# An attention kernel at one head and batch row per period: one load moved in ScalarE's queue, the weights' low parts given to GpSimd, and two planes made a stage earlier

## The reference

```python
x = x + _L0_cond_ref(x, adapter_ids, weight)      # x + x @ weight[id].T, per batch row
...
q = _rope(_rmsnorm(einsum('bsd,ed->bse', x, Wq), q_norm_w), pos)
k = _rope(_rmsnorm(einsum('bsd,ed->bse', x, Wk), k_norm_w), pos)
v = einsum('bsd,ed->bse', x, Wv)
k_all, v_all = [cached pages (512 keys), new keys (128)]
scores = einsum('bqhd,bkhd->bhqk', q, k_all) / sqrt(128); masked beyond the cached length
x = x + softmax(scores) @ v_all, through Wo
```

## Time and profile before

| what | us |
|---|---|
| median of 3 runs | 1062.12 |
| lowest and highest of them | 1061.57, 1069.5 |
| profiled execution, its own time | 1067.74 |
| its span in the trace | 1065.6 |
| TensorE busy in the span | 1021.3 |
| VectorE, ScalarE, GpSimd busy | 867.0, 804.7, 756.6 |

### The profile page before, as it was taken

One profiled execution on the slowest core, in us unless ns is written; L12 is line 12 of the kernel. 1 busy time (PEld: TensorE's weight loads), 2 busy tenths in 40 slices (PEclk: granted clock), 3 DMA queues, 4 the chain that ended last, 5 costly groups with the idle time before them and its releaser, 6 DMA issues.

```text
span 1065.6 us, 19559 instructions
## 1 busy us (share of the span) xinstructions
PE 1021.3 (96%) x5500; PEld 868.9 (82%) x5500; DVE 867.0 (81%) x1791; ACT 804.7 (76%) x2094; POOL 756.6 (71%) x794
## 2 busy tenths in 40 slices
PE   7899999999899999999999999999999999999996
PEld 5578788898788888888888888878888888788884
DVE  6566567676789999998898899998989989889892
ACT  4345456565788988888888888888888988898783
POOL 1767767665477777877877778777877868787663
PEclk9899999999999999999999999999999999999998
DMA  6689988896688899888898887988868788886874
GB/s 209 200 270 257 268 246 237 225 245 155 107 143 170 147 155 158 150 148 162 149 150 165 149 160 155 142 151 162 154 142 173 140 163 155 151 150 138 143 141 104
DMA packets 477501, 180.85 MB, mean 170 GB/s; under 512 B 420417, under 2 KB 457426, under 8 KB 475346
## 3 DMA queue, kind: packets, MB, share of 16 engines
q1 hardware_dynamic: 372480, 150.57, 68.7%
q10 hardware_dynamic: 103890, 26.94, 12.1%
q0 software_dynamic: 1024, 2.10, 0.7%
HBM read 109.25 MB, written 35.66 MB: 136 GB/s over the span
## 4 chain that ended last, share of the span: by engine, by line
PE 58%; DVE 11%; DMA 8%; SPq 7%; issue 6%; ACT 5%; POOL 4%; ACTq 0%; POOLq 0%; DVEq 0%
PE S L1225 13%; PE O L1158 5%; DMA turned<-pr 5%; PE O L1159 4%; PE O L1160 4%; PE Q L1158 4%; PE Q L1160 4%; PE Q L1159 4%; DVE pr L945 4%; PE T L1164 3%; SPq L405 3%; PE Y L1158 3%; PE Y L1159 3%; PE Y L1160 3%; DMA first<-pr 3%
## 5 line engine op out<-in xcount | busy, mean ns | idle before, releaser
L925 DVE CUSTOM_DVE_ANT_0 pr<-S,mask,rst 128x640 f32<-128x640 f32 x256 | 225.5, 881 | 43.0 <-PE S L1225 39.1
L945 DVE SCALAR_TENSOR_TENSOR pr<-pr,rc,raw 128x640 f16<-128x640 f32 x208 | 232.0, 1116 | 9.6 <-ACT raw L724 5.9
L739 ACT ACTIVATE pr<-pr,nb 128x640 f32<-128x640 f32 x256 | 211.4, 826 | 25.7 <-DVE nb L925 25.7
L541 POOL TENSOR_TENSOR m<-m 128x512 f32<-128x512 f32 x64 | 111.2, 1738 | 89.3 <-DVE m L973 87.3
L724 ACT ACTIVATE raw<-pr,rc 128x640 f16<-128x640 f32 x208 | 166.0, 823 | 5.1 <-DVE rc L941 5.0
L683 ACT ACTIVATE Q<-Q 128x128 f32<-128x128 f32 x256 | 68.2, 266 | 80.7 <-DVE m L973 80.7
L1225 PE MATMUL S<-kh,qh 128*128 128x320 f32 x512 | 122.4, 320 | 5.7 <-DVE nb L925 4.8
L1158 PE MATMUL O<-pth,vh 128*128 128x512 f32 x256 | 108.9, 425 | 15.5 <-POOL ptl L516 15.2
L516 POOL TENSOR_SCALAR ptl<-turned 128x512 fp32r<-128x512 f16 x130 | 94.1, 724 | 41.4 <-DMA turned<-pr 32.5
L495 POOL TENSOR_TENSOR kl<-raw,kh 128x512 fp32r<-128x512 f32 x64 | 92.5, 1446 | 43.1 <-ACT kh L623 42.6
L516 POOL TENSOR_SCALAR ptl<-first 128x512 fp32r<-128x512 f16 x130 | 99.1, 762 | 33.4 <-DMA first<-pr 23.1
(11 more groups left out here) (114 smaller groups left out, 2700.5 us busy)
## 6 DMA issues: line engine op xcount, KB each, us to landing
cache_rows<-in_kv SPq DMA_DIRECT2D x80, 256.0 KB, 4.9
wraw<-in_wall SPq DMA_DIRECT2D x73, 256.0 KB, 3.1
raw<-cache_rows SPq DMA_DIRECT2D x63, 256.0 KB, 3.1
raw<-cache_rows ACTq DMA_DIRECT2D x49, 256.0 KB, 4.4
cache_rows<-in_kv ACTq DMA_DIRECT2D x48, 256.0 KB
mask<-mask_rows SPq DMA_DIRECT2D x64, 128.0 KB
first<-in_lw SPq DMA_DIRECT2D x6, 1024.0 KB, 6.2
acc<-in_x SPq DMA_DIRECT2D x8, 256.0 KB
```

What stands on the lines that cost most here:

```text
L541: e.tensor_tensor(m1[:, :, :], m1[:, :, :], m2[:, :, :], ALU.add).then_inc(g_qadd, 1)
L739: e.activation(pr[:, slot(u, g), :], pr[:, slot(u, g), :], ACT.Exp, bias=nb[:, u % 2, g:g + 1], scale=-1.0, accum_out=sm[:, u % 2, g:g + 1 ...
L925: e.tensor_tensor_reduce(pr[:, slot(u, g), :].rearrange("p (a n) -> p a n", a=2), S[:, :, 0:320], mask[:, u % 2, :].rearrange("p (a n) -> ...
L945: e.scalar_tensor_tensor(out=lower16(u, g), in0=pr[:, slot(u, g), :], scalar=rc[:, u % 2, g:g + 1], in1=upper16[:, g, :], op0=ALU.mult, op ...
```

## The change

There are three edits. First, in the steady loop (periods 13 to 65) ScalarE's list has `load_k` behind `split_w(i, 0)` and `q_hi(j)`, which waits for TensorE's turned queries, instead of ahead of them. Second, from head 2 on chunk 5's low part, and from head 1 on chunk 8's, is made by GpSimd and no more by VectorE: chunk 5 one period later than before at place 0 behind chunk 4, chunk 8 one period later at place 0 ahead of chunk 9. These are 13 subtractions, 6 of chunk 5 and 7 of chunk 8. Third, in period 12 the planes of heads 0 and 1 of unit 12 (and the reciprocals that they need) are made inside the period and not at its end.

```diff
-LO_DVE = {(0, 6): (1, 1), (0, 7): (1, 1), (0, 9): (2, 1), (1, 4): (-2, 1),
-          5: (-2, 1), 8: (1, 1)}
+LO_DVE = {(0, 6): (1, 1), (0, 7): (1, 1), (0, 9): (2, 1), (1, 4): (-2, 1), (1, 5): (-2, 1)}
 LO_POOL = {(0, 8): (1, 1), 0: (-5, 1), 1: (-4, 1), 2: (-3, 0), 3: (-2, 1), 4: (-1, 0),
-           6: (0, 1), 7: (1, 0), 9: (2, 0)}
+           5: (-1, 0), 6: (0, 1), 7: (1, 0), 8: (2, 0), 9: (2, 0)}
...
                 split_w(i, 0)
+                if i == NA:
+                    upper_plane(i, 0)
                 if turn:
                     p_hi(w, 2)
...
+                if i == NA:
+                    upper_plane(i, 1)
                 if turn:
                     p_hi(w, 3)
...
-            for g in range(2):
-                upper_plane(NA, g)
-
...
-                if i + 2 < NU:
-                    load_k(e, i + 2)
                 split_w(i, 0)
                 if nxt:
                     q_hi(j)
+                if i + 2 < NU:
+                    load_k(e, i + 2)
...
                 new_v_lo(j)
+                if i == NA:
+                    scaled_recip(i, 0)
                 if i > 0:
                     largest(i, 2)
...
-                elif i == NA:
-                    scaled_recip(i, 0)
...
                 if i > 0:
                     largest(i, 3)
+                if i == NA:
+                    lower_plane(i, 0)
...
                 elif i == NA:
+                    lower_plane(i, 1)
                     scaled_recip(i, 1)
-                    lower_plane(i, 0)
-                    lower_plane(i, 1)
```

## The result

The median fell from 1064.88 us (4 runs of the kernel before, 1061.57 to 1069.5) to 1048.72 us (4 runs, 1044.97 to 1052.44). The ratio is 0.9845, with a 95% interval of 0.9814 to 0.9876: faster by 16.2 us, where the prediction had 18 off the median and 1044 us. The profiled execution took 1052.44 us, 15.3 less than that of before.

A forecast was written before the change was run, and what follows sets the result against it. TensorE, busy 96%, was taken as the bound, so only its lateness could be won. 17 + 4.1 + 3.4 - 3 = 21.5 us, taken as 18 off the 1062.1 us median, gave 1044 us; range 1035 to 1058.

The forecast's parts named there:

- The bound and the floor: Periods 13 to 62: TensorE bounds the kernel, a period's floor is 14.50 us, and the whole prize is 30.3 us.
- The load: Periods 14 to 62: issuing the key load later frees late last transposes; 22.3 us at stake, gain 17, bounds 0 and 22.
- I leave 5 us for them (about half caught): Periods 30, 33, 40, 54, 57: transposes issued at 8.1 to 8.5 us may still be caught, 1.8 to 2.2 us each.
- Gain 4.1: Periods 15, 39 and 47, late by VectorE: without chunk 5 there they should fall to the floor, 4.1 us together.
- cost 3: Six periods with b = 7: chunk 5 on GpSimd makes `m` late, 0.5 us each; cost 3 us, bounds 0 and 9.
- Planes: Unit 12's planes made earlier in period 12: period 13 falls from 18.40 to about 15; gain 3.4 us, bounds 1.5 and 3.9.
- the forecast's case: The whole kernel: the terms come out as forecast, 1044 us, with none of the rivals holding; chance 0.68.
- The first: Key load's move wins nothing, because load and transposes share the DMA engines whatever their order: 1058 us; chance 0.14.
- The second rival: Later load pushes the next unit's transposes back; some 15 periods then lose 1.8 us: 1062 us; chance 0.08.
- The third: GpSimd becomes the bound with b = 7, `m` 1.3 us or more late, costing 15 us: 1054 us; chance 0.06.
- The fourth: Keys come late, ScalarE waits in `kh` and transposes are caught by the next load: 1075 to 1086 us; chance 0.04.
- two signs of being wrong: Changed kernel's profile: `kh` waits for its load, or transposes still land over 4 us after issue in most periods.

The follow-up runs named there:

- experiment 1: The kernel before with only the key load moved behind the queries' high part: 1059.6 us, ratio 0.9943 to the kernel before.
- experiment 6: The changed kernel with chunk 5 given back to VectorE, chunk 8 staying on GpSimd: 1047.55 us, ratio 0.985 to the kernel before.
- experiment 8: The changed kernel with the key load behind the upper plane and chunk 5 halved between GpSimd and VectorE: 1040.68 us, ratio 0.978 to the kernel before.
- experiment 4: The changed kernel with the key load issued early, right behind the query squares: 1049.89 us, ratio 0.985 to the kernel before.

## Why the prediction was right, and where it was off

**The bound and the floor** held: 38 of the 49 periods of the changed kernel are at 14.50 to 14.53 us.

**The load.** The step that it would be issued at 8.8 to 9.3 us held (8.84 in the median); up to 9.9 it was late not with b = 6, as I wrote, but with b = 7, where `m` is late and `qh` with it. The limit of the last transpose near 7.95 held too: the four that were caught had been issued 8.0 to 8.13 us in. The keys landed at 12.2 to 13.9 us and `kh` waited nowhere. The size was off: I gave the term 17 us and it is 13.2 in the change's trace (20.1 lost by late transposes before, 6.9 after), 9.1 with the load alone. The step that sized it was "I leave 5 us for them (about half caught)". The five periods that I had named (30, 33, 40, 54, 57) all came down to 14.50 to 14.52 us, and four others were caught, at 1.63 us each. Which periods are caught is only in part a property of the period: 16, behind one with b = 7, is caught in every kernel that has the load at this place, 25 in three of four, the others change. That part cost 6.5 us, near the 5 that I left. What I had not counted: 2.2 of the 22.3 us were not this load's. Before, one late transpose of the 33 had a long lead, and 6 do in the changed kernel, and behind periods that are now short VectorE is late with b = 7, which longer periods ahead of them had hidden (experiment 1).

**Chunks.** "Gain 4.1" took periods 15, 39 and 47 to the floor, and "cost 3" then put 0.5 us on each of the six with b = 7. They stand 5.85 us above the floor together, 0.98 each, inside my bound of 9 and twice what I took: 15, 39 and 47 fell from 15.75, 16.09 and 15.73 only to 15.44, 15.44 and 15.61, 1.1 us in all. The two terms together were to give 1.1 us; by the lengths of the periods that VectorE or GpSimd's list made late (5.05 us lost in five of them before, 5.85 in six after) they gave -0.8, and against chunk 5 left where it was experiment 6 has no difference. `m` started where I had put it. What I had mis-sized is the cost to VectorE: the lower plane takes 0.9 us more (1.80 against 0.87 where it stands alone in the earlier trace rows), and what TensorE then waits for in period 39 is VectorE's row maximum, 0.7 us. With half a chunk there (experiment 8) the plane takes 1.30 us, all six such waits of TensorE together 1.1 us, and period 39 takes 14.94. That the one follows from the other is read from their order in the lists; GpSimd's list too runs without a wait to the first `p_lo`. Chunk 8, which I put at 0, was not moved alone in any run. The Trainium skill, SBUF — State Buffer, section SBUF: two separate sides, calls what the plane meets there an exclusive lock, and the rows agree.

**Planes.** Gain 3.4 forecast, bounds 1.5 and 3.9; period 13 gave 4.3 us, and period 12 took 0.3 back. The first `p_lo` there has no wait, as the prediction said. That it came out over the bound has two reasons. The bound took 14.50 us as the floor of period 13 too, but TensorE has 75 instructions there and not 82 and is busy for 13.41 us. And the prediction took the whole 18.40 us as waiting, while some 1.2 of the 4.3 us (by experiment 1) are the clock, which didn't fall any more.

**The sum.** In the stage from period 13 on it is 13.2 - 0.8 + 4.3 and 0.5 of small differences, 17.2 us, where 21.5 were forecast. The profiled executions differ by 15.3, with 3.2 us lost ahead of the stage and 1.0 won in the tail. On the median 18 forecast, 16.2 measured. That these two are so near is in part luck: the step from 21.5 to 18 rests on the assumption that the unprofiled runs have fewer late transposes, which no run shows, load and chunks gave 5.7 us less than forecast, and planes and small differences 1.4 more. The 1044 us also start from a median of 1062.1, which is 1064.9 with the fourth run. Two figures of the range don't fit its own terms: 30 us less than 1062 is 1032 and not 1035, and the chance of over 1% can't be 0.74 when the forecast's case has 0.68 and each rival stands above 1051.5 us.

**The rivals.** The first (load and transposes share the engines whatever their order) is refuted: the DMA share stayed at 0.84 while late transposes fell from 33 of 48 to 10, and with the load behind the upper plane it is higher, 0.86, with 7. The rule of the Trainium skill, DMA: Bandwidth & Descriptors, section Queues, rings and completion order (turns packet by packet), doesn't describe what the table shows, a step at 0.9 us of lead, which lies in the reports. It is nearer to experiment 4, where the data packets of transposes issued behind a load are slowed in nearly every period. The second rival holds in small: four new victims, not fifteen more. The third was half there (5.85 us, not 15). The fourth didn't occur. Of the two signs of being wrong neither showed: `kh` has no wait for its load, and 10 of 48 last transposes, not most, took over 3.5 us.

## What to carry to other kernels

Read a pipelined kernel period by period and ask of each late transfer what was issued just behind it, not how full the engines are: half a microsecond of order between a transpose that someone waits for and a bulk load that nobody needs yet decided 1.6 us of the period. A small transfer whose data has arrived can still be reported late, with the bulk load. Put the load behind the transpose, with a lead that holds in the latest period and not only in the typical one. And where two engines both lack the room for one whole piece, cut the piece: the period that was late with it on either side was nearly on time with half on each.

## What the runs showed that was not expected

Transposes with more than 0.9 us of lead still took 3.9 to 4.6 us in 6 of 44 periods (changed) and 7 of 48 (later load). At all of these places the trace has a packet of the instruction queue, of which there are 45 of 16 KB in the whole run, about one in 1.5 periods. In the six of the changed kernel it lasts 0.9 to 1.0 us and begins 1.2 to 2.6 us after the transpose's issue; in five of them the last data packet of the transpose begins at 3.1 to 3.3 us and not at 2.17. Three other such packets, which began 2.2 to 2.4 us after the issue, held up nothing. SyncE's issue of one transpose takes up to 2.7 us in place of 1.28 beside such a packet. That one follows from the other is read from their coincidence and was not tried.

A DMA that stands in ScalarE's list behind an activation is issued when the waits ahead of it are met, not when that activation is done: 626.90 ahead of `qh`'s 627.34 above, and at 5.3 us in experiment 4. Its place in the list is a place among waits.

A wait of TensorE can cost more than its length. In the steady loop of the eleven traces its clock fell to 1.2 GHz for 3.4 us in five places, each time in or behind a wait for `ptl` of 1.2 to 2.7 us; waits of 2.9 and 1.4 us in experiment 1 left it at 2.4 GHz. One such stretch made period 13 some 1.2 us longer.

Halving the load's bytes took 1.1 us off the 4.4 from its issue to its landing.
